# Weight block sums built in DRAM, and three pairs of cms chunks projected down by seven products a pair

## What is computed

```
# kind 1, twice (V = 512, H = 2048)
q, k, v  = x @ Wq, x @ Wk, x @ Wv
attn_out = softmax(q k^T * scale) v @ Wp + bp
cms_out  = gelu(attn_out @ cW1 + cb1) @ cW2 + cb2 + one_hot(code)
modifier = gelu(concat(attn_out, cms_out) @ mW1 + mb1) @ mW2 + mb2
x        = clip(x + cms_out + modifier, 0, 1)
# kind 2, twice: an adapter chosen by the sequence's role, and a layer norm
x = norm(x + gelu(x @ W_down[role] + b_down) @ W_up[role] + b_up) * gamma + beta
```

## Time and profile before

| | us |
|---|---|
| median of 3 runs (2156.2 to 2160.65) | 2157.89 |
| the profiled execution | 2156.44 |
| its span, first to last instruction | 2154.8 |
| PE busy in it, of 9256 MATMULs | 2105.6 (98%) |
| DVE, ACT, POOL busy | 1537.7, 1042.1, 598.7 |

### The profile page before, as it was taken

The page is one execution under the profiler, slowest core; times in us unless marked ns, Lnnn a source line. Parts: engine busy times, 40 slices in busy tenths (PEclk is TensorE's granted clock), DMA queues, the critical chain, the costliest instruction groups (busy, mean ns, idle before and its releaser), DMA issues.

```text
span 2154.8 us, 24846 instructions
## 1 busy us (share of the span) xinstructions
PE 2105.6 (98%) x9256; PEld 1724.7 (80%) x9256; DVE 1537.7 (71%) x1923; ACT 1042.1 (48%) x1527; POOL 598.7 (28%) x620
## 2 busy tenths in 40 slices
PE   8999999999999999999999999999999999999997
PEld 6888887888788887888877888788887888878884
DVE  4366678776867668876776766977686866787676
ACT  5264445454446444544554544444454644454444
POOL 1001136452001113655000111655400011355420
PEclk9999999999999999999999999999999999999999
DMA  8101131212202112221312111321130211311211
GB/s 304 40 10 59 59 88 49 59 48 78 100 20 88 59 59 69 59 59 59 116 41 88 40 59 42 96 59 59 40 127 20 102 46 59 88 50 59 59 59 39
DMA packets 125767, 146.41 MB, mean 68 GB/s; under 512 B 5952, under 2 KB 100160, under 8 KB 123728
## 3 DMA queue, kind: packets, MB, share of 16 engines
q1 hardware_dynamic: 122912, 130.05, 18.9%
q0 software_dynamic: 1504, 8.49, 1.9%
q10 hardware_dynamic: 1232, 6.29, 0.7%
HBM read 123.84 MB, written 12.58 MB: 63 GB/s over the span
## 4 chain that ended last, share of the span: by engine, by line
PE 85%; DVE 10%; ACT 2%; issue 2%; DMA 0%; SPq 0%; ACTq 0%; DVEq 0%
PE bank L615 28%; PE bank L617 28%; PE bank L616 28%; DVE ring L1321 2%; DVE vc L1363 2%; DVE pc L1493 1%; DVE xa L1358 1%; DVE lsum L1695 1%; ACT ring L955 1%; ACT raw L1098 0%; PE bank L923 0%; DVE xs L1700 0%; DVE xs L1653 0%; DVE xs L1685 0%; DVE raw L1439 0%
## 5 line engine op out<-in xcount | busy, mean ns | idle before, releaser
L1321 DVE TENSOR_TENSOR ring<-stage,ring 128x1024 fp32r<-128x1024 f32 (+1 forms) x312 | 363.4, 1176 | 103.8 <-ACT ring L955 103.6
L551 POOL TENSOR_TENSOR stage<-stage 128x256 f32<-128x256 f32 x120 | 106.3, 886 | 1122.1 <-DMA stage<-cms_w 904.5
L615 PE MATMUL bank<-ph_hi,ring 128*128 128x512 f32 x1048 | 410.6, 392 | 5.4 <-issue 2.4
L617 PE MATMUL bank<-ph_hi,ring 128*128 128x512 f32 x1048 | 407.9, 389 | 0.0
L616 PE MATMUL bank<-ph_lo,ring 128*128 128x512 f32 x1048 | 407.9, 389 | 0.0
L615 PE MATMUL bank<-xa,ring 128*128 128x512 f32 x1016 | 396.0, 390 | 2.9 <-DVE xs L1653 2.1
L617 PE MATMUL bank<-xa,ring 128*128 128x512 f32 x1016 | 395.3, 389 | 0.0
L616 PE MATMUL bank<-xa,ring 128*128 128x512 f32 x1016 | 395.3, 389 | 0.0
L955 ACT ACTIVATE ring<-stage 128x1024 fp32r<-128x1024 f32 (+1 forms) x312 | 296.3, 970 | 111.7 <-PE bank L617 78.3
L615 PEld LDWEIGHTS bank<-ph_hi,ring 128*128 128x128 f32 x1048 | 196.7, 188 | 53.7 <-issue 7.2
L617 PEld LDWEIGHTS bank<-ph_hi,ring 128*128 128x128 f32 x1048 | 196.7, 188 | 41.0
(11 more groups left out here) (159 smaller groups left out, 3139.6 us busy)
## 6 DMA issues: line engine op xcount, KB each, us to landing
stage<-mod_w SPq DMA_DIRECT2D x128, 256.0 KB, 3.4
stage<-cms_w SPq DMA_DIRECT2D x36, 512.0 KB, 3.6
stage<-mod_w SPq DMA_DIRECT2D x32, 512.0 KB, 4.9
stage<-cms_w SPq DMA_DIRECT2D x56, 256.0 KB, 4.3
fold_staging<-fold_w SPq DMA_DIRECT2D x16, 512.0 KB, 5.2
stage<-folded SPq DMA_DIRECT2D x16, 512.0 KB, 4.3
xs<-pc POOLq DMA_DIRECT2D x8, 1024.0 KB, 8.3
stage<-ada_w SPq DMA_DIRECT2D x16, 512.0 KB, 3.6
```

The lines of the kernel that those rows point to most:

```text
L551: pool.tensor_tensor(part(S1), part(S2), part(A22), ALU.add).then_inc(sums_ready, 1)
L615: pe.matmul(dst, lh, rh, start=start and n == 0, stop=False, skip_group_check=not start)
L617: done = pe.matmul(dst, ll, rh, start=False, stop=n == last, skip_group_check=not start)
L1321: dve.tensor_tensor(ring_part(key, 1), staged(key), f32(ring_part(key, 0)), ALU.subtract).then_inc(w_lo, 1)
```

## The change

Two things change.

**Sums in DRAM.** POOL's adds and the buffer's sums are gone. For each weight piece with seven products there is now a place in a DRAM tensor (`ready_w`, seven blocks of 128x256; `ready_pair`, seven of 128x512). `prepare` on ACT issues copies from the weights into it, DRAM to DRAM (4 for a piece A, C or D, 7 for a piece E). POOL then issues accumulating transfers within it (`sum_once`: 3 a piece, `sum_twice`: 2 a piece, a slot apart each), and SP loads all seven blocks with one transfer (`load_ready`). This is done once for each of the two layers: the pieces of slots 1 to 4 ahead of round 0, those of slots 5 to 15 of the first layer in slots 1 to 11 of round 0 (`AHEAD` = 4), and those of the second layer in slots 1 to 15 of round 1. Rounds 2 and 3 have none. ACT issues 282 copies in all: 30 ahead of round 0; in round 0 11, 4, 4 and 8 in slots 1 to 4 and 12 in each of slots 5 to 11; in round 1 11, 4, 11, 4, 11, 4, 4 and 8 in slots 1 to 8 and 12 in each of slots 9 to 15. They stand at the head of the slot in ACT's order. POOL issues 330 accumulating transfers.

**Pairs.** The down projections of cms chunks 0 and 1, 2 and 3, 4 and 5 are joined: two chunks of 256 are the two halves of a block product, done by seven products of four parts each (`pair_product`, 84 MATMULs a pair for 96). Its weights are the piece "E". The hidden tiles of a pair live in `raw` and `raw_odd`, POOL makes eight sums of 128x512 a pair (`pair_sum`), ACT and DVE split 14 tiles a pair for 8. Chunks 6 and 7 stay as they were.

The core of the diff:

```diff
-            def sums(key):
-                s, done, at = stage[STAGE_OF[key]], SUM_AT[key], DOWN_AT if key[1] == "D" else UP_AT
...
-                pool.tensor_tensor(part(S1), part(S2), part(A22), ALU.add).then_inc(sums_ready, 1)
-                pool.tensor_tensor(part(S3), part(S2), part(A11), ALU.add).then_inc(sums_ready, 1)
...
+            def sum_once(layer, slot):
+                pool.wait_ge(copied[slot], 16 * sum(COPIES[kind] for kind, _ in PREPARED[slot]) * (layer + 1))
+                for kind, n in PREPARED[slot]:
+                    w, at = ready_piece(layer, kind, n), UP_AT if kind in ("A", "C") else DOWN_AT
+                    for block, more in ((S1, A22), (S3, A11), (S4, A22)):
+                        pool.dma_start(w[:, at[block], :], w[:, at[more], :], accum_op=ALU.add).then_inc(summed_once[slot], 16)
...
+            def load_ready(key, slot):
+                layer, at = key[0] // 2, STAGE_OF[key]
+                to = stage_pair if key[1] == "E" else stage[at]
+                sp.wait_ge(w_lo, STAGE_FREE[key])
+                sp.wait_ge(prepared[slot], 32 * len(PREPARED[slot]) * (layer + 1))
+                sp.dma_start(to[:, :, :], ready_piece(layer, *key[1:])).then_inc(stage_in[at], 16)
...
+            def prepare(layer, slot):
+                for kind, n in PREPARED[slot]:
...
+                    for first in (at[S1], at[S3]):
+                        act.dma_start(to[:, first:first + 2, :].rearrange("p b (k n) -> p (b k) n", k=k // 2),
+                                      halves[:, :, 1, :]).then_inc(copied[slot], 16)
...
+            for early in range(1, AHEAD + 1):
+                prepare(0, early)
             fold_copy(3)
...
                 for n in range(1, SLOTS):
+                    if prepared_in(r, n):
+                        prepare(*prepared_in(r, n))
                     if n == CH:
...
+            def pair_even(r, n):
+                i = n // 2 - 1
+                up(r, n, Q5)
+                up(r, n, Q1)
+                pair_product(r, i, Q3)
+                up(r, n, Q6)
+                up(r, n, Q2)
+                up(r, n, Q3)
+                up(r, n, Q7)
+                pair_product(r, i, Q6)
+                up(r, n, Q4)
+            def pair_odd(r, n):
+                i = n // 2
+                for q in UP_ORDER[up_order(n)][:2]:
+                    up(r, n, q)
+                if i:
+                    pair_product(r, i - 1, Q7)
+                up(r, n, Q6)
...
```

More of the change, by code:

```diff
@@ L156, in staged_up @@
     def staged_up(r, n):
-        pieces.append(((r, "A", n), n % 2 if n < CH else 0))
+        pieces.append(((r, "A", n), 0))
         if n >= CH:
@@ L184, in weight_stream @@
         plain(r, "P", 0)
-        for n in range(CH):
-            if n and n - 1 not in LASTS:
-                down(r, n - 1)
-            up(r, n + 1, 0)
-            if n in LASTS:
-                down(r, n)
-            up(r, n + 1, 1)
+        up(r, 1, 0)
+        ops.append((r, "A", 1, 1))
+        for n in range(1, CH - 1):
+            if n % 2 == 0:
+                ops.append((r, "E", n - 1, 3))
+            if n > 1:
+                ops.append((r, "A", n, 1))
+            if n % 2:
+                pair_first(r, n)
+                ops.append((r, "E", n, 1))
+            up(r, n + 1, 0)
+            if n % 2:
+                ops.append((r, "E", n, 2))
+        ops.append((r, "A", CH - 1, 1))
+        down(r, CH - 2)
+        staged_up(r, CH)
+        ops.append((r, "A", CH, 0))
+        down(r, CH - 1)
+        ops += [(r, "C", CH, 0), (r, "A", CH, 1), (r, "C", CH, 1)]
         up(r, CH + 1, 0)
@@ L844, in down, with pair_product @@
                          (lambda k: pe.wait_ge(h_lo, hidden_at(r, n, k))) if b == 0 and m == 0 else None)
+            def pair_product(r, i, q):
+                blk, at = OPERAND[q], RING_E[q] * BLK
+                pe.wait_ge(w_lo, W_AT[r, "E", 2 * i + 1, PAIR_GROUP[q]])
+                pe.wait_ge(h_lo, pair_split_at(r, i, blk, 1))
+                before = {Q6: Q1, Q7: Q6, Q4: Q7, Q3: Q5, Q2: Q3}
+                if q in before:
+                    pe.wait_ge(added, pair_down_at(r, i, before[q]))
+                elif i:
+                    pe.wait_ge(added, pair_down_at(r, i - 1, Q4 if q == Q1 else Q2))
+                two = pair[int(q in (Q5, Q3, Q2))]
+                for j in range(2):
+                    tile(two[:, j, :], [(ring[:, 0, at + k * BLK + j * P:at + k * BLK + (j + 1) * P],
+                                         ring[:, 1, at + k * BLK + j * P:at + k * BLK + (j + 1) * P],
+                                         pair_hi(blk, k), pair_lo(blk, k)) for k in range(2)],
+                         down_done if j else None, start=q in (Q1, Q5, Q2))
@@ new lines, in pair_add @@
+            def pair_add(r, i, q):
+                b, m = DRAIN[q]
+                acc, src = pc[:, b, m:m + 2, :], pair[int(q in (Q5, Q3, Q2))]
+                minus = q in (Q5, Q7, Q4)
+                dve.wait_ge(down_done, pair_down_at(r, i, q))
+                if q not in PAIR_FIRST_DRAIN:
+                    dve.wait_ge(added, pair_down_at(r, i, {Q2: Q1, Q6: Q3, Q7: Q5}[q]))
+                elif i:
+                    dve.wait_ge(added, pair_down_at(r, i - 1, PAIR_LAST_DRAIN[b, m]))
+                if i == 0 and q in PAIR_FIRST_DRAIN:
+                    dve.wait_ge(attn_lo, (r + 1) * ATT_BUILDS)
+                    for j in range(2):
+                        done = dve.tensor_scalar(acc[:, j, :], src[:, j, :], -1.0 if minus else 1.0,
+                                                 cbias[:, 2 * r + b, m + j:m + j + 1], ALU.mult, ALU.add)
+                elif minus:
+                    done = dve.tensor_tensor(acc, acc, src[:, :, :], ALU.subtract)
+                else:
+                    done = dve.tensor_tensor(acc, src[:, :, :], acc, ALU.add)
+                done.then_inc(added, 1)
@@ L1593, in slot @@
-                up_lo(r, n + 1, 1)
-                if not last:
-                    for m in range(1, KT):
-                        down_add(r, n - 1, 1, m)
+                for m in range(KT):
+                    down_add(r, n - 1, 1, m)
+                hidden_lo(r, n, 3)
+                split_lo((r, "C", n + 1, 0))
+                hidden_lo(r, n, 1)
+                combine(r, n, C12)
+                hidden_lo(r, n, 2)
+                split_lo((r, "A", n + 1, 1))
+                split_lo((r, "C", n + 1, 1))
```

564 lines of the change are left out of this document (416 added, 148 removed).

## The result

The changed kernel takes **2419.9 us** (2415.7 to 2423.9, four runs), the kernel before in the same runs 2157.1: a ratio of **1.122**, 95% interval 1.120 to 1.124. The prediction was 2198 us with a range of 2137 to 2265. Its direction was right, its size wasn't: the loss is 263 us instead of 40, and the time lies far outside the range.

A forecast was written before the change was run, and what follows sets the result against it. PE was taken to bound the kernel, at 0.2266 us a MATMUL. 2156.4 - 32.6 (fewer MATMULs) - 8 (POOL's adds gone) + 72 (ACT's bursts) + 10 (the start) = 2198 us, range 2137 to 2265.

The forecast's parts named there:

- Fewer MATMULs: Pair slots: 84 MATMULs for 96 a pair, 144 fewer in all at 0.2266 us each, all on the path: -32.6 us.
- POOL's adds: Slot 8 and head of slot 9: without POOL's adds DVE's splits shorten and PE's gaps shrink; -8 us, between 0 and 11.8.
- New stalls in the pair slots: Odd and even pair slots: every operand arrives before its product, so 0; up to 1 us a pair, 12 us, for the range.
- POOL's issues: POOL, up to 15 issues a slot: they replace up to twelve adds, ahead of hidden sums with some 5 us of room; 0.
- ACT's issues at 0.65 us: ACT's queue: copies issued 0.65 us apart, priced from SP's rows of like shape; lower end 0.41.
- The bursts' term: Slot heads in rounds 0 and 1: ACT's bursts stop PE; 40 us in ten slots, 32 in the others, +72 us.
- The start: Ahead of round 0: 30 issues on ACT delay the first tiles that PE needs; +10 us, with 2 and 15 as ends.
- SP's larger loads: SP's loads: seven blocks for four cost some 1.4 us, less than the four adds that followed a load; taken as nothing.
- Rival 1: ACT's issues are cheap, 0.41 us each; bursts cost 23 us and the start 4; total 2143 us; chance 0.22.
- Rival 2: ACT's bursts back up, issues waiting for room, 10.5 us a burst; 122 us and the start 15; total 2253 us; chance 0.18.

The follow-up runs named there:

- the kernel without preparing: The changed kernel without copies and accumulating transfers, its seven-block loads reading other input of the same size: 2117.35 us, ratio 0.981.
- copies alone: The changed kernel without POOL's accumulating transfers; ACT issues all 282 copies and the loads wait for these only: 2262.84 us, ratio 1.049.

## Why the prediction was wrong

- **Fewer MATMULs, -32.6, and POOL's adds, -8.** Right: the kernel without preparing is 41.7 us faster (39.7 by the spans) for 40.6, and rounds 2 and 3 of the changed one are 9.8 and 8.7 us shorter, forecast 10. Part of the -8 was met by chance: slots 8 and 9 gave 9.0 us and the attention 2.8, while the new gaps of the next point took 4.4. The split named for slot 8 went from 1.595 to 1.224 us:

```profile
L1702 DVE TENSOR_TENSOR vc<-raw,vc 128x1024 fp32r<-128x1024 f32 x16 | 19.6, 1224 | 18.9 <-ACT vc L1208 18.8
```

- **New stalls in the pair slots, 0.** Nearly right, within the 12 us of the range: 1.1 us a round, in slots 1 and 2, also without preparing.
- **POOL's issues, 0.** This is the step that failed: 157 us of the 222 between forecast and measurement. "POOL's issues, up to 15 in a slot, replace up to twelve adds and stand ahead of hidden sums that have some 5 us of room" sets instruction against instruction without a price for the new one. The trace before had a near row, which I didn't use: POOL's own accumulating transfers for the residual (L585), 0.88 us each. By it 15 issues are 13.2 us, for some 10.7 of twelve adds (0.85 to 0.92 us each): a small cost. What it lacks, that POOL stands still between issues, is only hinted at in that trace: it stood still for 3.98 us between two of its small transfers at the start (L540, at 18.46 us). With room for three at a time the 15 are 28 us, and that is what failed. The rows of before can't give this number, but a range with 0 at both ends claimed that it was known. First the row of before, then that of POOL's issues now (ns min/median/max) and POOL's waits that nothing else in the profile explains:

```profile
L585 POOL DMA_DIRECT2D xs<-pc x8: 867/880/915, 309.1 to 1874.8; - x8
```

```profile
L677 POOL DMA_DIRECT2D ready_w<-ready_w x180: 804/1135/1482, 65.4 to 1388.7; - x180
```

```profile
POOL ready_w L677 <- issue: 257.2, 72, 12.5
```

- **ACT's issues at 0.65 us.** Right in most slots, medians of 0.638 and 0.648, and so was the mechanism, with its 3.6 us stop for 4.0. The row of one line, and its time to landing:

```profile
L1595 ACTq DMA_DIRECT2D ready_w<-mod_w x92: 540/638/2342, 237.1 to 1309.8; - x92
...
DMA to landing us min/median/max: 3.0/4.5/16.5
```

- **The bursts' term, +72.** Mis-sized: 132. A stop was priced by its length, while the clock that comes back only later adds about half of it again: 61 us for the ten slots instead of 40, 17 for slot 1 instead of 13, 33 for slots 3 to 7 instead of 19. And slot 8 was priced at nothing by the row of an idle ACT, where a burst on full transfer engines took twice its time: 21 us.
- **The start, +10.** 13.7 with copies alone, within its ends of 2 and 15. ACT's split came at 80.86 us where 81.4 had been worked out, but by luck: the 30 issues ended at 74.6 instead of 71.3, and the landing took 3.7 us instead of 7.7. With POOL's transfers beside them the split came at 89.28 and the cost was 16.9.
- **SP's larger loads, 0.** Right: the kernel without preparing has them and met the gain, and with SP's copies beside them they and the copies cost 3.5 us.
- **The rivals.** Rival 1's price of an issue wasn't met. Rival 2's issues that grow were real in slot 8, and mildly at the start (30 in 23.2 us for 19.5), not in the ten slots. Both rivals, and with them the range, turned on ACT's issues, and their price was the one that the rows gave best. The unknown lay on another engine.

What stays open: why single issues stretch in slot 8, which loses 20.9 us with the copies alone and 27.0 with POOL's transfers too; and whether still more room for descriptors would take the rest of POOL's pauses.

## What to carry to other kernels

A transfer is not free for the engine that issues it: count its issues as that engine's instructions, find who waits behind them, and give them to an engine, or a stretch, that nobody waits for. The same copies cost 146 us from ACT and 3.5 from SP, and sums of the second layer cost nothing in POOL's idle stretches, where ahead of a sum that others wait for they cost 157 with the first layer's. Where the trace of before has only a distant row for an added operation, or none, its price is the widest term of the sum, not the smallest.
